# Cross attention on one core: the transposes of a step's probabilities move from behind the next half's scores to in front of them

## What is computed

```python
q, k, v = heads(x @ Wq + bq), heads(ctx @ Wk + bk), heads(ctx @ Wv + bv)
score = einsum('bhqd,bhkd->bhqk', q, k) * scale
attn  = softmax(score, axis=-1)          # layer 0 adds a mask, layer 2 replaces masked scores
x     = x + merge(einsum('bhqk,bhkd->bhqd', attn, v)) @ Wo + bo
```

## Time and profile before

| | us |
|---|---|
| median of three runs (3988.9 to 3998.15) | 3998.14 |
| the profiled execution | 3992.23 |
| its span in the trace | 3990.4 |
| TensorE busy, matmuls | 3679.2 (92%) |
| turns, line 524, TensorE busy | 900.0 |
| keys, line 540, and values, line 554 | 691.8 and 701.0 |
| scores, line 512 | 459.3 |
| weighted values, line 569 | 396.9 |
| exponentials, line 789, ScalarE busy | 829.0 |
| maxima, lines 688 and 691, VectorE busy | 525.8 and 525.3 |

### The profile page before, as it was taken

One profiled execution on the slowest core, in us unless ns is written; L12 is line 12 of the kernel. 1 busy time (PEld: TensorE's weight loads), 2 busy tenths in 40 slices (PEclk: granted clock), 3 DMA queues, 4 the chain that ended last, 5 costly groups with the idle time before them and its releaser, 6 DMA issues. The chain is left out here.

```text
span 3990.4 us, 100284 instructions
## 1 busy us (share of the span) xinstructions
PE 3679.2 (92%) x42064; PEld 3200.4 (80%) x42064; DVE 2755.9 (69%) x7221; ACT 2155.5 (54%) x2988; POOL 1449.8 (36%) x1253
## 2 busy tenths in 40 slices
PE   7999999874999999988999999985998999999857
PEld 6888888643888888857888888864987888888647
DVE  6777777666777777753788888855447777777544
ACT  4565666455656656533455555533654656566434
POOL 3433333111322322130565555404873323222147
PEclk9999999996999999999999999987998999999978
DMA  3122224001111111010211121002542111110035
GB/s 99 51 68 55 55 52 129 25 17 37 47 39 35 43 43 35 10 41 16 77 62 59 51 68 58 28 13 100 200 148 79 35 39 43 39 35 26 13 113 181
DMA packets 125697, 235.81 MB, mean 59 GB/s; under 512 B 10032, under 2 KB 114880, under 8 KB 121408
## 3 DMA queue, kind: packets, MB, share of 16 engines
q1 hardware_dynamic: 118144, 175.58, 14.8%
q0 software_dynamic: 7104, 53.81, 3.9%
HBM read 208.39 MB, written 20.97 MB: 57 GB/s over the span
## 5 line engine op out<-in xcount | busy, mean ns | idle before, releaser
L640 ACT COPY prob_t<-ps 128x1024 f32<-128x1024 f32 x512 | 518.4, 1012 | 1044.8 <-PE ps L524 1044.8
L524 PE MATMUL ps<-c_ident,prob 128*128 128x128 f32 (+1 forms) x6656 | 900.0, 277 | 3.8 <-ACT prob_t L640 3.0
L524 PEld LDWEIGHTS ps<-c_ident,prob 128*128 128x128 f32 (+1 forms) x6656 | 733.9, 141 | 137.5 <-issue 122.4
L789 ACT ACTIVATE prob<-prob,nmx 128x1601 f32<-128x1601 f32 x512 | 829.0, 1627 | 1.1 <-DVE nmx L697 1.1
L554 PE MATMUL ps<-wv,ctx 128*128 128x256 f32 x4992 | 701.0, 289 | 0.0
L540 PE MATMUL ps<-ctx,wk 128*128 128x400 f32 (+1 forms) x3072 | 691.8, 361 | 4.9 <-DVE ctx L665 2.9
L554 PEld LDWEIGHTS ps<-wv,ctx 128*128 128x128 f32 x4992 | 618.5, 185 | 2.8 <-issue 2.8
L688 DVE CUSTOM_DVE_ANT_0 prob<-ps,mk 128x400 f32<-128x400 f32 (+2 forms) x1024 | 525.8, 569 | 40.6 <-PE ps L512 28.2
L540 PEld LDWEIGHTS ps<-ctx,wk 128*128 128x128 f32 x3072 | 535.2, 191 | 16.8 <-issue 7.6
L691 DVE TENSOR_SCALAR_CACHE_REDUCE prob<-ps 128x400 f32<-128x400 f32 (+2 forms) x1024 | 525.3, 569 | 8.0 <-PE ps L512 6.7
L640 DVE COPY prob_t<-ps 128x1024 f32<-128x1024 f32 (+1 forms) x384 | 401.3, 1045 | 123.8 <-PE ps L524 123.5
(11 more groups left out here) (346 smaller groups left out, 4261.8 us busy)
## 6 DMA issues: line engine op xcount, KB each, us to landing
raw_ctx<-in_ctx_t SPq DMA_DIRECT2D x120, 400.0 KB, 3.3
raw_ctx<-in_ctx_t SPq DMA_DIRECT2D x60, 402.0 KB, 5.0
raw_ctx<-in_ctx_t SPq DMA_DIRECT2D x60, 399.0 KB, 3.2
mk<-in_mask_f SPq DMA_DIRECT2D x32, 400.2 KB, 5.4
mk<-in_mask_i SPq DMA_DIRECT2D x16, 800.5 KB, 4.4
sorted<-zeros SPq DMA_DIRECT2D x2, 3840.0 KB, 19.9
rows<-sorted SPq DMA_DIRECT2D x30, 256.0 KB, 8.6
done<-done SPq DMA_DIRECT2D x30, 256.0 KB, 2.5
```

What stands on the lines that cost most here:

```text
L524: mm = pe.transpose(ps[0:w, turn_bank(u, i) + a, r * P:(r + 1) * P], prob[u % 2][:, r, x * P:x * P + w], cst['ident'][:])
L640: copy(prob_t[0:w, place(2 * i):place(2 * i) + nb, :], ps[0:w, turn_bank(u, i):turn_bank(u, i) + nb, :]).then_inc(st[sem], 1)
L789: a.activation(prob[h % 2][:, r, :], prob[h % 2][:, r, :], ACT.Exp, bias=nmx[:, r:r + 1], accum_out=den[h % 2][:, r:r + 1]).then_inc(st['e ...
```

## The change

In TensorE's list of work the call of `turn(u, i)` moves ahead of `scores(u + 1, i)`, and so ahead of `weighted(u - 1, x)` too in step 0. The instructions are the same, and so are their waits; the lists of the other engines are untouched.

```diff
         for u, i, attend, score, chunk, pairs in steps():
+            if attend:
+                turn(u, i)
             if score:
                 scores(u + 1, i)
             if u >= 1 and i == 0:
                 for x in weighted_late:
                     weighted(u - 1, x)
-            if attend:
-                turn(u, i)
             if u >= 1 and i == 1:
                 spread_denominators(u - 1)
             if 6 in pairs:
```

## The result

The changed kernel takes 4159.69 us (median of three runs, 4153.03 to 4162.14), against 3998.14 before. The ratio is 1.0412, with a 95% interval of 1.0397 to 1.0426. The forecast was 4186 us, in a range of 4110 to 4230. The profiled execution took 4153.03 us with a span of 4151.2, which is 160.8 more than before's 3990.4.

What follows compares the result with a forecast made beforehand. TensorE's list bounds the old kernel; in the new order a loop through the exponentials sets the period. Periods +174, first periods +6 and last halves +8 were put at +189 us in total, forecast 4186 us, range 4110 to 4230.

Steps and rivals of the forecast that it cites:

- TensorE's list bounds the stage, and the exponentials end after the scores begin: Cross attention, old order: TensorE always busy; exponentials end 0.58 or 1.28 us after step 0's scores begin.
- The loop sets the period: Turn 0 to fourth scores, maxima, exponentials, next turn 0: 23.22 us a half, 23.37 in layer 2.
- the first term: TensorE from the start of turn 0 to the start of the fourth scores, layers 0, 1 and 3: 13.43 us.
- The sum: 29 longer periods in four layers +174 us, first periods +6, last halves +8: total +189 us.
- The first period: Half 0 to half 1 in each layer: grows by about 1.5 us, four times, +6.
- The last halves: Half 31, turn now ahead of half 30's weighted values: +2.1 us in each of four layers, +8.
- TensorE's own list grows by about 0.4 a half: TensorE's work without waits: from 21.6 to 21.9 us to some 22.1 a half, below the loop's 23.2.
- Both orders switch the tiling mode equally often: TensorE's list: two switches a step, three in step 0, in both orders; by the skill's rule, order itself costs nothing.
- rival B: Order costs nothing: turns keep 0.85 us, loop shrinks to 22.44, 22.59 in layer 2; 4093 us, chance 0.10.
- Rival C: Clock falls behind the wait: turn and scores there at half clock, +186 us on top, 4372 us; chance 0.02.
- Rival D: Loop catches the collision of VectorE's output write with GpSimd's queries: up to 0.56 us each half, 4251 us; chance 0.07.
- Rival A: Faster: collision delay avoided (about 14 us), keys and values before turns cheaper (31 us): 3953 us; chance 0.03.

Runs made afterwards that it cites:

- the row waits: Changed kernel, but in the turn of step 0 each row of heads' two transposes wait for that row's exponential only: 4074.69 us, ratio 1.0204.
- the fourth experiment: Changed kernel with exponentials of 801 instead of 1601 columns: 4004.38 us, ratio 1.0030 to the kernel before.
- the second and third experiments: Kernel before with only step 0's turn in front: 4141.18 us; kernel before with step 0's turn between scores and weighted values: 4063.45 us.
- the last experiment: Kernel before with ScalarE's masking of the next queries ahead of its copy of step 1's turn: 3981.32 us, ratio 0.9969.
- the fifth experiment: Kernel before with exponentials of 801 instead of 1601 columns: 3993.04 us, ratio 0.9995.

## Why the prediction was right, and by how much its terms were off

- *TensorE's list bounds the stage, and the exponentials end after the scores begin.* Right: 124 waits of 1.14 us, where "some 120 times, about 1.1 us each" was forecast. Four experiments vary the cover (all of it, none, 0.75 us, shorter exponentials), and the loss follows it.
- *The loop sets the period.* Right: even and odd halves are equal, and so they are with the row waits, at a lower level. The period is 22.98 to 23.00 instead of the 23.22 forecast, and 23.23 in layer 2 instead of 23.37. The difference is all in the first term, 13.13 us and not 13.43. The mis-sized price is that of a turn in front of scores. I took the 1.02 us of rows 7 for all four; it holds for the turn behind the wait, but behind keys or values it is 1420.82 - 1419.85 = 0.97. These three turns make 0.15 of the 0.30, and the sign that a turn in front of scores takes 1.02 everywhere did not hold. The turn of rows 7 also stands *behind* a tiled group (a group whose matmuls use 32 rows or 32 columns of the array), which the sum took no notice of. And nothing is added behind scores, where I had taken 0.10: keys take 1.20 there, as in front of a turn anywhere. The 0.05 for the wait into TensorE is 0.06 by its own rows, 3701.07 and 3701.13, and 0.06 here.
- *The sum.* 29 periods in four layers: 666.9 + 666.4 + 673.7 + 666.3 less 2523.6 = +149.7 us, against 174 forecast. The first period of each layer adds 5.2 (6 forecast; 20.0 us instead of 18.6 in layers 0, 1 and 3). The last halves, forecast as 8, take 6.6 more (1.2 in layers 0, 1 and 3 and 3.0 in layer 2, from step (30, 0) to the last spread), and everything outside 0.7 less.
- *TensorE's own list grows by about 0.4 a half.* Too much: 0.12, or 0.28 in layer 2.
- *Both orders switch the tiling mode equally often*, on which rival B rested: not so in layer 2. There, in the old order, the 32 weighted matmuls of step 2 run straight into the fourth scores, from column tiles to row tiles. In the new one a turn stands between them, one switch more. In the fourth experiment's trace (layer 2):

```profile
2297.98 1.08 PE L569 MATMUL ps<-prob_t,vals 128*32 128x128 f32 x32
2298.99 1.09 PE L524 MATMUL ps<-c_ident,prob 128*128 128x128 f32 x8
2300.01 0.82 PE L512 MATMUL ps<-keys,q_parts 32*128 32x400 f32 x12
```

  Layer 2 pays 0.16 us a half more than layer 0. Start to start, 0.06 of it is in the turns (this one takes 1.02, the others 0.97), 0.06 in the keys (those of step 2 stand in front of weighted values in both orders and get no cheaper), and the rest in scores and values. The Trainium skill (TensorEngine Tiling (Array Packing), Key Properties) says that a change of the tiling mode drains TensorE. The 0.05 more of this turn is in that direction; that the switch is its cause is not shown. With an equal number of switches, 0.12 are left in layer 0, so the neighbours count too.
- *Rival B* (4093): wrong. A turn in front of scores does take 0.12 to 0.17 us more than elsewhere. On TensorE's own list cheaper keys and values make up for most of that, which is why the order by itself is nearly free; but the loop holds four such turns in full, and only three of the cheaper groups. *Rival C*: the clock stayed at 1.00. *Rival D*: the collision did not enter the loop. The longest write of the outputs in layers 0, 1 and 3 is 0.29 us, and GpSimd is through 0.59 us before it, where 0.6 was forecast. It did enter it in the second and third experiments. In layer 2 nearly all of these writes take more than 0.4 us, before and after (up to 1.77 and 0.89 us); its fourth scores take 0.75 to 0.90 before and 0.76 after. *Rival A*: its 14 us for the collision are real, and the last experiment got them without the change.

## What to carry to other kernels

Here one engine was saturated, and the order of its list was worth little by itself (0.1 to 0.3 us in 22). But each wait in such a list has a cover: the work between the point where the other engine's result could first be asked for and where it is. Before moving a waiting instruction forward, read when its releaser ends against the start of what it is moved past; and then close the loop through the engine waited for, since its sum, not the engine's load, gives the new period. If such a wait has to stand there, split it to the granularity of what is read; here that gave back half of the loss.

## What was not expected

The collision of VectorE's output write with GpSimd's query parts turns on thousandths of a microsecond. In layers 0 and 3 of the kernel before VectorE's write starts 37 to 45 ns ahead of GpSimd's instruction (rows 9 are one of these cases); it takes 0.85 us, and GpSimd's 0.73. In layer 1 it starts 48 or 49 ns ahead; it takes 0.285 us, and GpSimd's 0.83. So the two meet in all three layers, and a few nanoseconds go with which of them is held up. Why the line lies there is not shown. The same list of TensorE falls on either side of it in different layers, and in different builds. In layer 1 of the kernel before VectorE was never the one held up (627.3 us for 29 halves). In the fifth experiment, which shares its order and has shorter exponentials only, it is in 11 halves, where it starts 46 or 47 ns ahead, and is not in three, where it starts 49 ahead:

```profile
L512 PE MATMUL ps<-keys,q_parts x1396: 332/341/450, 1033.2 to 1665.8; 32*128 32x400 f32 x149, 32*128 32x402 f32 x51
...
L735 DVE SCALAR_TENSOR_TENSOR XNT<-both,cols x29: 283/285/855, 1043.0 to 1653.6; 128x64 f32<-128x64 f32 x29
```

632.6 us there, 5.3 more. The kernel before ranges from 3987.16 to 4000.34 us over 16 runs, and the last experiment from 3979.22 to 3983.97 over six. I take it that part of this range is how many layers fall on the wrong side; only single profiles were seen, so this is argued and not shown.
